# Weights turned and split inside the first batch, and the last batch's end inside its steps, in a one-core attention and gating kernel

## What is computed

```
xn = layernorm(x)
q, k, v = xn @ Wq.T (16 heads of 64), xn @ Wk.T, xn @ Wv.T (4 heads of 64)
att = softmax(q k / 8, masked: causal, the last 512 keys, and the first 4 keys always)
s = (att v) @ Wo.T
thought = layernorm(xn)[last token] @ agg_w + agg_b
4 times: thought += gelu(layernorm(thought) @ d1_w + d1_b) @ d2_w + d2_b
broadcast = thought @ bc_w + bc_b
gate = sigmoid(xn @ gate_w + gate_b)
out = x + s * silu(layernorm(xn + gate * broadcast))
```

## Time and profile before

| what | us |
|---|---|
| median of 3 runs (2361.39 to 2364.69) | 2362.84 |
| the profiled execution | 2364.85 |
| its span, first to last instruction | 2363.1 |
| PE busy | 2234.7 (95%) |
| DVE busy | 1457.7 (62%) |
| ACT busy | 853.9 (36%) |
| HBM read and written | 297.37 MB and 79.72 MB |

### The profile page before, as it was taken

The page is one execution under the profiler, slowest core; times in us unless marked ns, Lnnn a source line. Parts: engine busy times, 40 slices in busy tenths (PEclk is TensorE's granted clock), DMA queues, the critical chain, the costliest instruction groups (busy, mean ns, idle before and its releaser), DMA issues. The chain is left out here.

```text
span 2363.1 us, 35786 instructions
## 1 busy us (share of the span) xinstructions
PE 2234.7 (95%) x13576; PEld 1643.1 (70%) x13576; DVE 1457.7 (62%) x3060; ACT 853.9 (36%) x1826; POOL 154.0 (7%) x376
## 2 busy tenths in 40 slices
PE   3699999999999999999999999994999999999998
PEld 3567666676666676666676766652788888888887
DVE  2545656646557656566665566563576676667666
ACT  2125554435455444455443545452111111111111
POOL 0200001100000100000100000000011011001100
PEclk6799999999999999999999999995999999999999
DMA  8683547834545853344863344346334333433431
GB/s 320 232 265 109 174 148 225 246 103 139 172 130 187 272 167 107 131 150 148 263 214 109 130 145 153 137 143 236 128 135 133 121 119 133 140 107 127 142 113 66
DMA packets 183293, 379.11 MB, mean 160 GB/s; under 512 B 20888, under 2 KB 119256, under 8 KB 167280
## 3 DMA queue, kind: packets, MB, share of 16 engines
q1 hardware_dynamic: 176112, 354.07, 45.4%
q0 software_dynamic: 5120, 16.85, 2.1%
q10 hardware_dynamic: 1920, 6.29, 0.8%
HBM read 297.37 MB, written 79.72 MB: 160 GB/s over the span
## 5 line engine op out<-in xcount | busy, mean ns | idle before, releaser
L706 ACT ACTIVATE pt<-t_ps 128x512 f32<-128x512 f32 x480 | 265.8, 595 | 530.3 <-PE t_ps L937 528.5
L871 PE MATMUL j_ps<-x_hi,w 128*128 128x512 f32 x1216 | 408.8, 405 | 0.0
L715 ACT ACTIVATE probs<-probs,neg_max 128x644 f32<-128x644 f32 (+5 forms) x512 | 352.8, 694 | 48.5 <-DVE neg_max L1150 48.4
L1150 DVE CUSTOM_DVE_ANT_0 probs<-s_ps,mask 128x644 f32<-128x644 f32 (+5 forms) x512 | 316.6, 655 | 83.2 <-PE s_ps L908 78.6
L937 PE MATMUL t_ps<-ident,probs 128*128 128x128 f32 x1920 | 270.2, 280 | 7.8 <-ACT pt L706 4.7
L1511 PE MATMUL out_ps<-wo,by_hi 128*128 128x512 f32 x1024 | 273.7, 389 | 0.0
L871 PEld LDWEIGHTS j_ps<-x_hi,w 128*128 128x128 f32 x1216 | 228.1, 190 | 52.7 <-issue 6.5
L908 PEld LDWEIGHTS s_ps<-k_hi,q 64*128 64x128 f32 x1536 | 145.9, 185 | 170.4 <-issue 95.9
L908 PE MATMUL s_ps<-k_hi,q 64*128 64x512 f32 (+4 forms) x1536 | 243.7, 352 | 8.0 <-DVE q L1128 5.6
L937 PEld LDWEIGHTS t_ps<-ident,probs 128*128 128x128 f32 x1920 | 208.2, 141 | 48.4 <-issue 15.9
L871 PE MATMUL j_ps<-x_lo,w 128*128 128x512 f32 x608 | 241.6, 397 | 0.0
(11 more groups left out here) (169 smaller groups left out, 2655.8 us busy)
## 6 DMA issues: line engine op xcount, KB each, us to landing
fw<-in_L_ffn_d_w_dram SPq DMA_DIRECT2D x128, 1024.0 KB, 5.2
w<-WT SPq DMA_DIRECT2D x48, 1024.0 KB, 5.1
xn<-in_L_attn_x_dram POOLq DMA_DIRECT2D x32, 512.0 KB, 5.5
XS<-x_hi SPq DMA_DIRECT2D x32, 512.0 KB, 7.4
XS<-x_lo SPq DMA_DIRECT2D x32, 512.0 KB, 8.5
Y<-y SPq DMA_DIRECT2D x256, 64.0 KB, 2.2
b_x<-in_L_attn_x_dram SPq DMA_DIRECT2D x32, 512.0 KB, 4.3
b_y<-Y SPq DMA_DIRECT2D x32, 512.0 KB, 6.4
```

The costliest lines, as they stand in the source:

```text
L706: act.activation(pt[:, m % PT_SLOTS, :, :], bank[:, :].rearrange("p (h q) -> p h q", q=P), ACT.Copy).then_inc(pt_ready, 1)
L715: act.activation(probs[:, slot, 0:width], probs[:, slot, 0:width], ACT.Exp, bias=neg_max[:, slot:slot + 1], scale=-1.0, accum_out=row_sum[ ...
L871: last = pe.matmul(bank_of((kind, b, n)), w[:, slot, wp * C + c * P:wp * C + c * P + P], xs[:, c, bass.ts(ch, BANK)], start=i == 0, stop=i ...
L1150: dve.tensor_tensor_reduce(out=probs[:, slot, 0:width], in0=s_ps[head % 2][:, 0:width], in1=m, scale=-SCALE, scalar=-NEG, op0=ALU.add, op1 ...
```

## The change

- **prepare_weights is gone.** Five tiles (Wv 0 and 1, Wk 0, Wq 0 and 1, `FIRST`) are turned and split in attend's start, amid its loop over x, straight into the buffer `w` from which the products read. The other seven (`LATER`) are turned in steps 2, 4, 6, 10, 12, 18 and 20 of batch 0, at the place where later steps turn x (`turn_later`, `turned_high`, `turned_low`). All twelve are also stored to WT, which batches 1 to 3 load from as before. Batch 0 loads none from WT.
- **The start.** x is loaded five tiles ahead (POOL), into buffers that the steps use later. ACT issues the loads of the first three weight tiles. The small vectors come as rows, and one transpose turns them (`turn_vectors`). Masks are built later on POOL. The stores of batch 0's x_hi and x_lo move into steps 1 to 8, one tile a step.
- **The last batch.** Its feed-forward tiles stand closer (up to two a step from step 10 and from step 20 on), the sum of the thought comes in step 27, its turn in step 28, the bc_w tiles in steps 29 and 30 and their fold in step 31. gate_w is loaded into xn and split into x_hi and x_lo in steps 26 to 31 (`GATE_AT`), and the split x of output tiles 0 and 1 is loaded into `w` (`load_ahead`).
- **finish** shares x_hi, x_lo and w with attend. It loads and turns only Wo, with the gate product of tile 0 around the first four tiles of Wo. gate_ps is doubled, and PE makes the gate product of tile t + 1 ahead of the output product of tile t.

The diff, cut to its core:

```diff
-def prepare_weights(nc, WT, Wq, Wk, Wv):
...
-        TILES_AT = {s: [] for s in range(UNITS)}
-        for t in range(D1_TILES):
-            TILES_AT[2 + t].append(t)
-        for t, s in enumerate((19, 20, 21, 22, 22, 23, 23, 24, 25, 26, 26, 27, 28, 29, 30, 31)):
-            TILES_AT[s].append(D1_TILES + t)
-        HIDDEN_AT = {2 + KB: 0, 2 + D1_TILES: 1}
-        SUMS = sum(1 for s in TILES_AT if TILES_AT[s])
+        TILES_AT = [{s: [] for s in range(UNITS)} for _ in range(B)]
+        for b in range(B - 1):
+            for t in range(D1_TILES):
+                TILES_AT[b][2 + t].append(t)
+            for t, s in enumerate((19, 20, 21, 22, 22, 23, 23, 24, 25, 26, 26, 27, 28, 29, 30, 31)):
+                TILES_AT[b][s].append(D1_TILES + t)
+        for t, s in enumerate((2, 3, 4, 5, 6, 7, 8, 9, 10, 10, 11, 11, 12, 12, 13, 14, 16, 17, 18, 19, 20, 20, 21, 21,
+                               22, 22, 23, 23, 24, 24, 25, 26, 29, 29, 30, 30)):
+            TILES_AT[B - 1][s].append(t)
+        HIDDEN_AT = [{2 + KB: 0, 2 + D1_TILES: 1}] * (B - 1) + [{2 + KB: 0, D1_TILES - 1: 1}]
+        FOLD_AT, TURN_AT, BC_FOLD_AT = 27, 28, 31
+        GATE_AT = {26: (0,), 27: (1, 2), 28: (3,), 29: (4, 5), 30: (6,), 31: (7,)}
         def sums_before(b, s):
-            return SUMS * b + sum(1 for n in range(s) if TILES_AT[n])
+            return sum(1 for n in range(UNITS * b + s) if TILES_AT[n // UNITS][n % UNITS])
...
+        FIRST = (V0, V0 + 1, K0, 0, 1)
+        LATER = {2: 2, 4: 3, 6: K0 + 1, 10: 4, 12: 5, 18: 6, 20: 7}
+        LATER_NO = {t: n for n, t in enumerate(LATER.values())}
+        LATER_STEP = list(LATER)
+        ORDER = [("w", t, half) for t in FIRST[0:2] for half in range(2)]
         for t in range(TB + 1):
             if t < TB:
                 ORDER += [("x", 0, 2 * t), ("x", 0, 2 * t + 1)]
             if t >= 1:
                 ORDER.append(("v", 0, t - 1))
+            if t == 1:
+                ORDER += [("w", FIRST[2], half) for half in range(2)]
             if t == 5:
                 ORDER.append(("k", 0, 0))
+        ORDER += [("w", t, half) for t in FIRST[3:] for half in range(2)]
         ORDER += [("k", 0, 1), ("q", 0, 0), ("q", 0, 1)]
         EARLY = len(ORDER)
         for b in range(B):
...
+                        if b == 0:
+                            if s in LATER:
+                                store_weights(LATER[s])
+                            if s - 1 in LATER_STEP[:-2]:
+                                load_raw(LATER_STEP.index(s - 1) + 2)
+                            if 1 <= s < 1 + TB:
+                                store_x(0, s - 1)
+                        if b == B - 1:
+                            if s == 24:
+                                for k in range(2):
+                                    load_gate(k)
+                            if s == 26:
+                                load_ahead()
+                            if s == FOLD_AT:
+                                sp.wait_ge(thought_ready, 2 + 2 * B)
+                                sp.dma_start(bias_rows, bc_b.partition_broadcast(B)).then_inc(bias_loaded, 16)
+                            for k in GATE_AT.get(s, ()):
+                                if k + 2 < KB:
+                                    load_gate(k + 2)
                         if b + 1 < B:
...
+                def load_x(b, t):
+                    if b == 0:
+                        if t >= 5:
+                            pool.wait_ge(j_full, NUMBER["x", 0, 2 * (t - 5) + 1] + 1)
+                        pool.dma_start(x_in(0, t), x[0, bass.ts(t, P), :]).then_inc(first_x_loaded[t % 5], 16)
+                        return
+                    if t >= 2:
+                        pool.wait_ge(x_full, x_half(b, 2 * (t - 2) + 1) + 1)
+                    elif b == 1:
+                        pool.wait_ge(x_full, 2 * (len(LATER) - 2 + t) + 2)
+                    else:
+                        pool.wait_ge(x_full, x_half(b - 1, 2 * (TB - 2 + t) + 1) + 1)
+                    pool.dma_start(x_in(b, t), x[b, bass.ts(t, P), :]).then_inc(x_loaded[t % 2], 16)
+                for t in range(5):
+                    load_x(0, t)
...
+                        for k in GATE_AT.get(s, ()):
+                            act.wait_ge(j_full, NUMBER["q", B - 1, 4 * KV - 1] + 1)
+                            act.wait_ge(xs_stored, 32 * TB * B)
+                            act.wait_ge(raw_gate_loaded[k % 2], 16 * (k // 2) + 16)
+                            act.activation(x_hi[:, k, :], xn[k % 2], ACT.Copy).then_inc(gate_high, 1)
...
+                def turn_weights(i):
+                    t = FIRST[i]
+                    pe.wait_ge(first_raw_loaded[i], 16 if i < 3 else 32)
+                    for half in range(2):
+                        wait_bank(("w", t, half))
+                        for c in range(4):
+                            last = pe.transpose(bank_of(("w", t, half))[:, bass.ts(c, P)],
+                                                first_raw[i][:, bass.ts(4 * half + c, P)], ident[:, :])
+                        last.then_inc(j_full, 1)
+                def turn_vectors():
+                    pe.wait_ge(small_loaded, 16 * 5)
+                    pe.transpose(f_ps[:, 0:4 * KB + HB], vec_rows, ident[0:4 * KB + HB, 0:4 * KB + HB]
+                                 ).then_inc(vec_turned, 1)
...
+                turn_weights(0)
+                turn_weights(1)
                 for t in range(TB + 1):
                     if t < TB:
                         turn(0, 2 * t)
                         turn(0, 2 * t + 1)
+                    if t == 0:
+                        turn_vectors()
+                    if t == 1:
+                        pe.wait_ge(vec_ready, 1)
+                        turn_rows(0)
                     if t >= 1:
                         v_proj(0, t - 1)
-                    if 1 <= t < 1 + AGG_TILES:
-                        if t == 1:
+                    if t == 1:
+                        turn_weights(2)
+                    if 2 <= t < 2 + AGG_TILES:
+                        if t == 2:
                             pe.wait_ge(cols_ready, 1)
-                        square_tile(t - 1, t - 1, AGG_TILES)
+                        square_tile(t - 2, t - 2, AGG_TILES)
                     if t == 5:
                         proj("k", 0, 0, 0, STEPS)
+                    if t == 6:
                         fold_rows(0)
+                turn_weights(3)
+                turn_weights(4)
                 proj("k", 0, 1, 0, STEPS)
                 turn_rows(1)
...
+                    if b == B - 1 and s == FOLD_AT:
+                        add_rows(B, thought, thought)
+                        dve.wait_ge(thought_ready, 2 + 2 * B)
+                        dve.tensor_copy(t_rows, thought).then_inc(t_rows_ready, 1)
+                    if b == B - 1 and s == TURN_AT:
+                        dve.wait_ge(f_turned, 2 + B)
+                        dve.tensor_copy(cols_view[:, 0:KB, :], f_cols.rearrange("p (k b) -> p k b", b=B)
+                                        ).then_inc(cols_ready, 1)
+                    if b == B - 1 and s == BC_FOLD_AT:
+                        dve.wait_ge(bias_loaded, 48)
+                        add_rows(1 + B, t_rows, None)
...
+                        for k in GATE_AT.get(s, ()):
+                            dve.wait_ge(gate_high, k + 1)
+                            dve.tensor_tensor(x_lo[:, k, :], xn[k % 2], x_hi[:, k, :].bitcast(F32),
+                                              ALU.subtract).then_inc(gate_split, 1)
...
                 for n in range(O_TILES):
-
-                    i = 2 * n + 1
-                    pe.wait_ge(raw_loaded[i % RAW], 16 * (i // RAW) + 16)
+                    if n == 0:
+                        gate(0, 0, range(KB // 2))
+                    if n == O_TILES // 2:
+                        gate(0, 0, range(KB // 2, KB)).then_inc(gate_done, 1)
+                    pe.wait_ge(raw_loaded[n % RAW], 16 * (n // RAW) + 16)
                     if n >= 2:
-                        pe.wait_ge(w_lo_ready, i - 3)
+                        pe.wait_ge(w_lo_ready, n - 1)
                     for c in range(KB):
-                        last = pe.transpose(wo_ps(n)[:, bass.ts(c, P)], raw[i % RAW][:, bass.ts(c, P)], ident[:, :])
+                        last = pe.transpose(wo_ps(n)[:, bass.ts(c, P)], raw[n % RAW][:, bass.ts(c, P)], ident[:, :])
                     last.then_inc(wo_turned, 1)
-                pe.wait_ge(w_lo_ready, WEIGHTS)
 
                 def body(t, s, pair, group):
-                    pe.wait_ge(z_ready, after(t))
-                    pe.wait_ge(xs_loaded[s], 32 * pair + 32)
-                    products(gate_ps, x_hi[s], x_lo[s], parts[0], parts[1]).then_inc(gate_done, 1)
+                    if follows(t, 1):
+                        pe.wait_ge(z_ready, after(t))
+                        pe.wait_ge(xs_loaded[1 - s], 32 * (pair + (s == 1)) + 32)
```

(2 more changed lines are left out.)

551 lines of the change are left out of this document (295 added, 256 removed).

## The result

The changed kernel takes 2297.9 us (median of four runs, 2295.8 to 2301.2) against 2363.4 us before on the same chip: a ratio of 0.9725, 95% interval 0.9708 to 0.9742, 65.4 us faster. Forecast were 2294, between 2272 and 2316: the number held. Its terms did not hold equally well. The profiled execution of after took 2301.2 us in all, with a span of 2299.5. The profiled execution of before has a span of 2363.1.

The account below looks back on a forecast made before the run. The matrix engine was taken as full in attention steps and gated output, idle or half-clocked at the start and between them. Terms -54 + 8.5 + 17 - 24.7 - 20.8 + 5 = -69.0 us gave 2294, range 2272 to 2316.

Parts of the forecast that it names:

- The start (-54): Up to batch 0's first scores: first transposes at 16.5 us, first scores at 95, 54 us earlier.
- Rival A: Start: fed too slowly, about 7 MB requested at once; x last, transposes at 25 us, total 2303; chance 0.14.
- The bound of 107: Start, slow bound: first scores at 107 us, with all idle kept and half clock for the additions (42 earlier).
- Rival F: Weights prepared inside a loop that the vector engine bounds, start ending at 107 us: total 2306; chance 0.05.
- Batch 0 (+8.5): Batch 0's steps: seven weight tiles at 0.95 us make 6.7, with waits up to 13; 8.5 us taken.
- The last batch (+17): Last batch's steps: 5.5 us feed-forward tiles, 4.3 in step 27, 6 other low parts, 1.2 last fold; bounds 10 and 26.
- Behind attention (-24.7): Between attention and gated output: the last y store becomes the last thing, next part at 1595.7 us; gain 24.7.
- The last part (-20.8 and +5): Gated output: 721.9 us against 742.7, gain 20.8; then 5 us lost in the loop, mainly tiles with bc loads.
- Rival C: Last part's loop is bound by vector engine and loads, costing 28 us instead of 5: total 2317; chance 0.08.
- D: Last part: every tile as slow as the bc tile, 24.3 us each, total 2368, slower than before; chance 0.03.
- B: Work in full steps costs more than its length: batch 0 at 13, last batch at 26, total 2308; chance 0.13.
- E: Less cost: start at its bound of 87 us, steps at 6.7 and 10, total 2277; chance 0.13.

Follow-up runs that it names:

- experiment 5: Changed kernel, with ScalarE issuing the first three raw weight loads only once the small token-row load has landed: first scores at 97.0 us.
- experiment 9: Changed kernel, start: from the third tile, next x's statistics stand ahead of low parts on the vector engine: first scores 92.25 us, first copy of y 106.36.
- experiment 2: Changed kernel, leaving out seven eighths of each low part of the seven weight tiles in batch 0's steps: batch 0 is 3.1 us shorter.
- experiment 1: Changed kernel, with two weight tiles moved from step 10 to 9 and 18 to 19 of batch 0: 2295.7 us, ratio 0.9717.
- experiment 3: Changed kernel, leaving out fifteen sixteenths of each of the eight gate-weight low parts in the last batch: last batch 315.4 us instead of 321.4.
- experiment 4: Changed kernel, with the last batch's eight gate-weight low parts on GpSimd instead of the vector engine: last batch 316.0 us, 5.4 less.
- 12: Changed kernel, with two weight tiles moved (steps 10 to 9, 18 to 19) and the gate's low parts on GpSimd: 2294.0 us, ratio 0.9707 to before.
- experiment 11: Changed kernel, with the last part's load of x for tile t+2 issued 1.2 us later: the part takes 749.7 us, 27.8 more.
- experiment 10: Changed kernel, with each gate again directly ahead of its output product and Wo's turns before gate 0: last part 727.6 us, 5.7 more.

## Why the prediction was right, and where it was wrong

**The start (-54): mechanism right, 2 to 4 us short.** The first transposes came at 18.1 instead of 16.5. The failed term is the load of the token rows, for which 1 us of sharing was allowed: it took 3.5 us more than when it is alone (experiment 5), which put the token chain's end at 14.5 instead of 11.8. Of these 2.7 us 1.1 came back, since the low parts of the first weights fell into the wait for the first x's statistics and not behind it. Rival A named this mechanism and put it on x; x was not late. From there to the first scores 78.5 us were forecast and 78.5 measured, but not by the terms as written: PE's work was 72.0 us rather than 70, because all of it up to 32 us ran at the lower rate, and the waits were 6.4 rather than 8.5. First scores at 96.6, that is -52.4; in the other runs 95.3 to 97.0 (but for experiment 9). Between the first scores and the first copy of y another 2.8 us went to the clock in the profiled execution. The bound of 107 does not follow from the terms beside it: with the idle time kept and the additions doubled they give 102. Rival F rests on it and would stand at 2301; nothing else does.

**Batch 0 (+8.5): wrong in size.** Measured +15.4, above the bound of 13, and +14.0 to +18.4 in the ten executions with this code. The failed step is "7 x 0.95": the transposes are 1.04 a tile, but the wait for the bank comes in every tile and the wait of the next turn of probabilities for the low part in four of the seven (2.1 together, experiment 2), and I had them only in the bound. And the list of what lies in which step was not read for collisions: step 10's tile stands ahead of the sum of the hidden rows in the vector engine's queue, which is 1.7 us of wait and up to 2.8 of lower clock behind it (experiment 1). The stores, raw loads and feed-forward loads on SP cost nothing, as forecast.

**The last batch (+17): the sum right, +16.9, two of its pieces by luck.** The six tiles more up to step 24 came to 5.8 (forecast 5.5), the steps from 26 on to 10.7 for 11.5 (and 0.4 at the batch's start). Step 27 is as forecast. It was to be 4.3 us longer (by the prediction's own terms 5.2 less a gap of 1.2, so 4.0) with the vector engine over 90% busy; it is 4.0 longer, and the vector engine is busy for 10.52 of 10.77 us:

```profile
1515.18:1525.95 10.77, 6.45 (x47) 3.91 (x46) 10.52 (x24) 7.28 (x15) 0.00 (x0) 1.00 0.63 240
```

Step 28 is 3.8 longer where 1.0 was forecast, 2.5 of it the lower clock (experiment 3). The two terms of step 31, a low part and the last fold (2.2 together), did not come: the step is as long as before, and what follows it 1.1 shorter. The two errors cancel. The low parts cost 3 to 7 us (experiments 3, 4 and 12) against some 8 in the sum. GpSimd as the place for the low parts (experiment 4) confirms that it is the vector engine's order, not its total work.

**Behind attention (-24.7): -23.75.** The last copy of y to the next part is 4.7 us; the 3.8 forecast had left out the BC store that still follows on SP (0.84).

**The last part (-20.8 and +5): the first right to a tenth, the second wrong.** The part takes 721.9 us as forecast, gate 1 begins 24.6 us into it (forecast 25). The +5 for tiles with a bc load did not come. The failed step is that each late tile was added up by itself. Read from the code, the vector engine may be late with y's low part by most of a gate product (10.9 us) before PE waits. What counts is the mean over tiles, and tiles of 21.9 to 22.5 with a bc load between others of 21.4 to 21.9 have a mean of 21.77 (the 30 behind the first), with 21.76 PE's own. Rival C and D were right on the other side of that line: with 1.2 us more in the load the mean is 22.7 and the part 27.8 us longer (experiment 11). The prediction had credited the order of the products with nothing in the loop, and experiment 10 agrees: the order is worth 5.7 us, none of them in the loop.

**The sum** came out closer than its terms, and that is luck: an error of +6.9 in batch 0, one of +4.4 in the start (to the first copy of y) and +1 behind attention met one of -5 in the last part and -1.8 in batches 1 and 2, for which nothing was forecast. Of the 1.8, 1.0 is the granted clock in one step (step 24 of batch 1, above). Together the forecast was 5.4 us too low in the span, 3.9 in the median.

**Rivals.** B (work in full steps costs more than its length) is the one that the runs bear out for batch 0, and for a reason that it did not name: not load, but two fixed waits and one collision in an in-order queue. E did not happen in any of its three terms (first scores at 96.6 and not 87, steps +15.4 and +16.9), and F did not happen.

## What to carry to other kernels

Work moved into a full step costs its own length plus the waits that it brings to the two queues that it crosses; read these off a step that already holds such work, and check each target step for an instruction that another engine waits for behind the new one. A late stage in a loop with buffers is to be judged by its mean over the period of the buffers, not tile by tile. And a gain in front of a stretch with short waits may be taken back by the granted clock (it was in the one execution of experiment 9): measure it at the next fixed point, not where it arises.

## What the hardware showed

- A wait of PE of 1 to 2 us in a full stretch was followed, in some executions and not in others, by a granted clock of 0.75 to 0.87 over the step: 9.14, 10.73 and 11.89 us for the same 64 products. The two levels are 2.4 and 1.2 GHz. The Trainium skill, "TensorE: Matmul & The Clock Gate", section "A second HAM failure mode: psum-queue depth-cycling", describes short idle times between groups of products that make the clock go back and forth; the rows agree that such idle times matter, and show a spread between executions of equal code.
- The granted clock also fell without a wait: from 528.6 us on in before, at the end of 16 products of four columns, with PE busy throughout. The same stretch took 10.07, 8.77 and 7.44 us at 0.66, 0.81 and 1.00.
- PE's rate stayed up across an idle time of 2.7 us for eight more transposes (0.66 for four) and was down for what followed (24.35), while an idle time of 5.6 us was followed by the lower rate at once.
- GpSimd's subtraction of 128x1024 took 2.38 us, 1.22 on the vector engine. The Trainium skill, "GPSIMD Engine Reference", section "3.1 Elementwise — side-by-side cycle accounting", gives about 2.6 cycles an element at 1.2 GHz; an estimate from that, 1024 x 2.6 / 1.2 = 2.2 us, is near it.
